# Attention scores by pairs of heads: the query's high and low part stacked on 128 rows, 128-column matmuls, and the last weight groups split at another place

## The chip, the cores and the metric

The kernel runs on one core of a Trainium2 chip. The metric is the device time of one execution in microseconds (us), the median of three runs: 1743.74 us before the change. Engines are named as the profile names them: PE (matmul, with PEld for its weight loads), DVE (vector), ACT (scalar), POOL (GpSimd) and SP, which issues nearly all the DMAs.

## The reference, cut to what matters

Two attention layers run one after the other. The change lies in the first: 4 x 1024 tokens of width 1024 look at 4 x 64 context rows, with 32 query heads of 32 columns and 8 key/value heads, each shared by 4 query heads.

```python
q = hidden_state @ Wq + bq                # 4096 x 1024
k = encoder_hidden_state @ Wk + bk        # 256 x 256
v = encoder_hidden_state @ Wv + bv
scores = jnp.einsum('bkgld,bksd->bkgls', q, k) * scale + mask
attn = jax.nn.softmax(scores, axis=-1)
out = jnp.einsum('bkgls,bksd->bkgld', attn, v)
x = layernorm(out @ Wo + bo + hidden_state) * gamma + beta
```

The second layer is an attention of 16 heads with 64 keys on x and the same context. The kernel keeps float32 accuracy by splitting each operand of a product into a high part, rounded to the TensorE's float32r type, and a low part (the rest), and adding three matmuls: high by low, low by high, high by high.

## The kernel before, in words

The first layer's attention is cut into 64 units (`UNITS`): a unit is one block of 512 tokens and one key/value head with its four query heads, so 128 rows of query. Eight units with the same tokens follow each other. Every engine runs one loop over slots `u`, written out by hand with semaphores; a slot holds steps of several units at once:

- PE, slot u: the query projection of unit u (`query`: 8 pieces of 3 matmuls of 512 columns, the helper `three`, whose lines are L53 to L55), between its pieces the product of attention and values of unit u-4 (`values_of`, 6 matmuls of 512 columns), and, behind piece 6, the scores of unit u-1: for each of 4 groups of 128 tokens one `three` of 256 columns, 12 matmuls. `qs` (the query, high and low tile) is the stationary side, `kb` the moving one. `kb` is block diagonal: head j's rows hold the keys in head j's 64 columns and zeros elsewhere.
- ACT: the exponential of unit u-2, the rounding of the next tokens' tile (`xT`), the copy of a finished output (`ot`), `qs` high from PSUM with the bias added (L869), then the rounding of the turned probabilities (`pT`).
- DVE: the sum of the exponentials of unit u-2 (L1107), a reciprocal, in even slots the turning of an input tile (L1040), the masked scores of unit u-1 out of PSUM (L1127) and their maximum (L1133), the turned probabilities of unit u-2 (L1138), `qs` low (L1142, `SCALAR_TENSOR_TENSOR`); in odd slots the low part of the input tile (L1047) comes first.
- POOL: low part of `pT` (L1381), scaling (L1385) and centering (L1390) of the probabilities.

PE waits for `qs` low of unit u-1 before its scores. One pair of slots (an even and an odd one) holds one input tile.

Ahead of the units the keys are rounded into `kst` (ACT the high plane at L839, DVE the low one at L1087), stored to DRAM (L288), and loaded for each unit into `kb` (L301, four DMAs, one for each head). The weight of the query projection `wq` comes in 8 column groups; a group is split by ACT (L793) and DVE (L1059) where `wq_early` and `wq_late` say, the last two in slot 1. The output projection's weight `wo` is split in the same way in the slots 57 to 64 (`wo_groups`; DVE L1064), and from slot 64 on `half_tile` multiplies by it: its second half waits for all 8 groups.

## Time and profile before

| what | value |
|---|---|
| median of 3 runs | 1743.74 us (1743.04 to 1747.58) |
| the profiled execution's own time | 1745.89 us |
| its span, first to last instruction | 1744.1 us |
| PE busy | 1712.8 us (98%), 8449 matmuls |
| DVE, POOL, ACT busy | 1165.5 (67%), 1066.8 (61%), 581.5 us (33%) |
| granted PE clock, mean | 0.995 |

The chain of work that ended last is 72% PE, 9% DVE, 8% POOL. A matmul's recorded time holds its way through the array; how fast matmuls follow each other is read from their starts. The units lie between about 31 and 575 us; behind them come the output projection with layer norm, the second layer's tables, and the second layer.

### The profile page before, as it was taken

Reading aid. Unit: us, or ns where it says so; the run is one execution under the profiler, and the core shown is the slowest. Engines: PE = TensorE matmul, PEld = TensorE weight load, DVE = VectorE, ACT = ScalarE, POOL = GpSimd, SP = SyncE. Lnnn points to the kernel's source line nnn. Section 1 sums busy time; section 2 is a strip of 40 time slices with the busy share of each in tenths; the row PEclk is TensorE's granted clock in tenths of the full one; section 3 lists DMA queues with packets and bytes.
Section 4 is the critical chain, followed back from the end, with each engine's and each line's share of the span. In section 5 each row is a group of like instructions: output and inputs, shape, how many; then the busy total and the mean of one; then the engine's idle time right before and its main releaser. Section 6 shows DMA issues by size and latency. Waiting matters only on the chain.

```text
span 1744.1 us, 22384 instructions
## 1 busy us (share of the span) xinstructions
PE 1712.8 (98%) x8449; PEld 1429.8 (82%) x8449; DVE 1165.5 (67%) x1106; ACT 581.5 (33%) x669; POOL 1066.8 (61%) x592
## 2 busy tenths in 40 slices
PE   6999999999999999999999999999999999999998
PEld 6788888888888788888888877888888888888887
DVE  7899888888888666565656578446644664466443
ACT  4344454444444533333434223122312231223110
POOL 1677878777788966575756553445734573457331
PEclk9999999999999999999999999999999999999999
DMA  8342344323335677777776856556545654565332
GB/s 238 99 111 73 88 104 105 85 71 86 80 81 162 198 237 223 227 231 222 248 219 224 263 176 194 174 169 185 173 152 169 185 170 154 169 183 171 130 110 84
DMA packets 278127, 280.11 MB, mean 161 GB/s; under 512 B 62330, under 2 KB 230404, under 8 KB 278020
## 3 DMA queue, kind: packets, MB, share of 16 engines
q1 hardware_dynamic: 276672, 276.97, 52.3%
q10 hardware_dynamic: 1348, 1.71, 0.3%
q8 instruction: 67, 1.10, 0.3%
q14 instruction: 40, 0.33, 0.1%
HBM read 175.81 MB, written 102.76 MB: 160 GB/s over the span
## 4 chain that ended last, share of the span: by engine, by line
PE 72%; DVE 9%; POOL 8%; issue 4%; ACT 3%; DMA 2%; SPq 1%; POOLq 0%; DVEq 0%; ACTq 0%
PE ps L53 23%; PE ps L54 23%; PE ps L55 23%; POOL pT0l L1381 2%; POOL pr L1385 1%; PE ps L712 1%; PE ps L720 1%; POOL xb L1407 1%; DVE pT1r L1138 1%; DVE pr L1127 1%; DVE small L1107 1%; DVE pT0r L1138 1%; ACT pT1h L881 1%; DVE xT1r L1040 1%; DVE xT0r L1040 1%
## 5 line engine op out<-in xcount | busy, mean ns | idle before, releaser
L1458 POOL TENSOR_TENSOR x2Tl<-x2r,x2Th 128x1024 fp32r<-128x1024 f32 x31 | 74.6, 2405 | 274.2 <-ACT x2Th L973 274.2
L1235 DVE STREAM_TRANSPOSE x2r<-xd 128x1024 f32<-128x1024 f32 x32 | 68.9, 2154 | 200.1 <-PE ps L55 200.1
L1390 POOL TENSOR_TENSOR pr<-pr,small 128x1024 f32<-128x1024 f32 x64 | 122.0, 1906 | 98.6 <-DVE small L1133 98.5
L973 ACT CAST x2Th<-x2r 128x1024 fp32r<-128x1024 f32 x32 | 33.7, 1053 | 366.5 <-DVE x2r L1235 366.5
L1385 POOL TENSOR_TENSOR pr<-pr,small 128x1024 f32<-128x1024 f32 x64 | 122.0, 1906 | 8.7 <-DVE small L1111 6.2
L1407 POOL TENSOR_TENSOR xb<-xb,bo 128x1024 f32<-128x1024 f32 x32 | 77.9, 2436 | 69.2 <-DMA xb<-in_x_dram 69.2
L1107 DVE TENSOR_REDUCE small<-pr 128x16 f32<-128x1024 f32 x64 | 78.0, 1219 | 45.7 <-ACT pr L852 45.7
L1421 POOL TENSOR_TENSOR y<-y,bet 128x1024 f32<-128x1024 f32 x31 | 74.4, 2400 | 55.7 <-DVE y L1153 55.7
L53 PE MATMUL ps<-wo0h,oc0l 128*128 128x512 f32 x256 | 101.7, 397 | 1.7 <-DVE wo0l L1064 1.7
L1153 DVE TENSOR_TENSOR y<-y,gam 128x1024 f32<-128x1024 f32 x32 | 56.0, 1751 | 70.6 <-ACT y L894 70.6
L53 PE MATMUL ps<-wo0h,oc1l 128*128 128x512 f32 x256 | 101.6, 397 | 0.4 <-DVE y L1190 0.4
L53 PE MATMUL ps<-xT0h,wq0l 128*128 128x512 f32 x256 | 100.8, 394 | 1.1 <-DVE wq0l L1059 1.1
L54 PE MATMUL ps<-xT0l,wq0h 128*128 128x512 f32 x256 | 100.7, 393 | 0.0
L55 PE MATMUL ps<-xT0h,wq0h 128*128 128x512 f32 x256 | 100.1, 391 | 0.0
L53 PE MATMUL ps<-xT1h,wq0l 128*128 128x512 f32 x256 | 100.0, 391 | 0.0
L54 PE MATMUL ps<-xT1l,wq0h 128*128 128x512 f32 x256 | 100.0, 391 | 0.0
L54 PE MATMUL ps<-wo0l,oc0h 128*128 128x512 f32 x256 | 99.8, 390 | 0.0
L54 PE MATMUL ps<-wo0l,oc1h 128*128 128x512 f32 x256 | 99.8, 390 | 0.0
L55 PE MATMUL ps<-wo0h,oc0h 128*128 128x512 f32 x256 | 99.7, 390 | 0.0
L55 PE MATMUL ps<-wo0h,oc1h 128*128 128x512 f32 x256 | 99.7, 390 | 0.0
L55 PE MATMUL ps<-xT1h,wq0h 128*128 128x512 f32 x256 | 99.6, 389 | 0.0
L1381 POOL TENSOR_TENSOR pT0l<-pT0r,pT0h 128x1024 fp32r<-128x1024 f32 x32 | 92.1, 2880 | 8.8 <-ACT pT0h L881 8.8
(379 smaller groups left out, 5446.3 us busy)
## 6 DMA issues: line engine op xcount, KB each, us to landing
xr<-in_x_dram SPq DMA_DIRECT2D x128, 128.0 KB, 2.9
o_scratch<-ot SPq DMA_DIRECT2D x256, 64.0 KB, 1.8
ocr<-o_scratch SPq DMA_DIRECT2D x16, 1024.0 KB, 7.9
xb<-in_x_dram SPq DMA_DIRECT2D x32, 512.0 KB, 6.2
a_scratch<-ost SPq DMA_DIRECT2D x64, 256.0 KB, 3.4
b_scratch<-ost SPq DMA_DIRECT2D x64, 256.0 KB, 5.6
xd<-x_scratch SPq DMA_DIRECT2D x128, 128.0 KB, 2.9
raw<-b_scratch SPq DMA_DIRECT2D x64, 256.0 KB, 5.9
```

Source lines behind the costliest of these rows:

```text
L53: nc.tensor.matmul(out, a[1], b[0], start=start, stop=False)
L54: nc.tensor.matmul(out, a[0], b[1], start=False, stop=False)
L55: return nc.tensor.matmul(out, a[0], b[0], start=False, stop=stop)
L1107: nc.vector.tensor_reduce(sm, pr[v % 2][:].rearrange("p j m s -> p (j m) s"), AX_X, ALU.add)\
L1153: nc.vector.tensor_tensor(y[n % 3][:], y[n % 3][:], gam0[:], ALU.mult).then_inc(scaled, 1)
L1235: nc.vector.transpose(x2r[:].rearrange("p k (t j) -> p t k j", t=TPB), xd[:].rearrange("p t (i k) -> p t k i", k=KT)).then_inc(x2_turned, 1)
L1381: nc.gpsimd.tensor_tensor(pT[v % 2][1][:], pTr[v % 2][:], f32(pT[v % 2][0][:]), ALU.subtract).then_inc(p_lo, 1)
L1385: nc.gpsimd.tensor_tensor(heads(v), heads(v), rs.unsqueeze(2).to_broadcast([P, TPB * GRP, KEYS]), ALU.mult)\
L1390: nc.gpsimd.tensor_tensor(heads(v), heads(v), mx.unsqueeze(2).to_broadcast([P, TPB * GRP, KEYS]), ALU.subtract)\
L1407: nc.gpsimd.tensor_tensor(xb[n % 2][:], xb[n % 2][:], bo0[:], ALU.add).then_inc(xbo, 1)
L1421: nc.gpsimd.tensor_tensor(y[n % 3][:], y[n % 3][:], bet0[:], ALU.add).then_inc(normed, 1)
L1458: nc.gpsimd.tensor_tensor(x2T[1][:], x2r[:], f32(x2T[0][:]), ALU.subtract).then_inc(x2_lo, 1)
```

## The change

The query tile of a unit is no longer a high and a low tile of four heads. Tile a holds heads 0 and 1: their high part on rows 0 to 63, their low part on rows 64 to 127. Tile b holds heads 2 and 3: high on rows 64 to 127, low on rows 0 to 63. ACT writes the two high halves and DVE the two low halves, with the low half going to the other 64 rows. Scores are formed by pairs of heads: for each of 4 token groups and each pair two matmuls of 128 columns, the first with low keys under the high rows only, the second with high keys under all rows. That is 16 matmuls of 128 columns in place of 12 of 256. `kst` has four planes (low, high, high, low), `kb` four planes of two heads, and each load of `kb` brings three planes.

The split of `wq` groups 6 and 7 goes from slot 1 to slots 3 and 5. The split of `wo` group 7 goes from slot 64 to slot 63.

```diff
-        kst = [at(f"kst{h}", 136 + 2 * h, [P, BATCH, 2, KEYS], F32R) for h in range(2)]
+        kst = [at(f"kst{h}", 130 + 4 * h, [P, BATCH, 4, KEYS], F32R) for h in range(2)]
-        kb = [at(f"kb{i}", 160 + 2 * i, [P, GRP, 2, KEYS], F32R) for i in range(2)]
+        kb = [at(f"kb{i}", 160 + 2 * i, [P, 4, 2, KEYS], F32R) for i in range(2)]
         def wq_late(u):
-            return (4, 5) if u == 0 else (6, 7) if u == 1 else ()
+            return (4, 5) if u == 0 else (6,) if u == 3 else (7,) if u == 5 else ()
         def wo_groups(u):
-            return (u - (UNITS - 7),) if UNITS - 7 <= u <= UNITS else ()
+            return (u - (UNITS - 7),) if UNITS - 7 <= u < UNITS else ()
...
                 for j in range(GRP):
-                    sp.dma_start(f32(kb[u % 2][32 * j:32 * (j + 1), j]).rearrange("p x s -> p (x s)"),
-                                 d["kv"][g // 4, t // 2, :, g % 4, :P]).then_inc(k_ld[u % 2], 16)
+                    x = 1 - j // 2
+                    sp.dma_start(f32(kb[u % 2][32 * j:32 * (j + 1), x:x + 3, j % 2]),
+                                 d["kv"][g // 4, t // 2, :, g % 4, KEYS * x:KEYS * (x + 3)].rearrange("p (x s) -> p x s", x=3))\
+                        .then_inc(k_ld[u % 2], 16)
...
                     for m in range(TPB):
-                        last = three(nc, S[v % 2][:, 256 * m:256 * (m + 1)], [qs[v % 2][x][:, m] for x in (0, 1)],
-                                     [kb[v % 2][:, :, x] for x in (0, 1)], True, True)
+                        for h in range(2):
+                            for x in (3 - 3 * h, 1 + h):
+                                last = nc.tensor.matmul(S[v % 2][:, 256 * m + P * h:][:, :P], qs[v % 2][h][:, m],
+                                                        kb[v % 2][:, x].rearrange("p j s -> p (j s)"), start=x in (0, 3), stop=x in (1, 2))
...
-                    nc.scalar.activation(qs[u % 2][0][:], Q[u % 2].rearrange("p (n m) -> p m n", m=TPB), ACT.Identity,
-                                         bias=bq[:, u % KT:u % KT + 1]).then_inc(q_hi, 1)
+                    for h in range(2):
+                        own = slice(64 * h, 64 * (h + 1))
+                        nc.scalar.activation(qs[u % 2][h][own], Q[u % 2][own].rearrange("p (n m) -> p m n", m=TPB), ACT.Identity,
+                                             bias=bq[own, u % KT:u % KT + 1]).then_inc(q_hi, 1)
...
-                    dve.wait_ge(q_hi, u + 1)
-                    nc.vector.scalar_tensor_tensor(out=qs[u % 2][1][:], in0=Q[u % 2].rearrange("p (n m) -> p m n", m=TPB), scalar=bq[:, u % KT:u % KT + 1],
-                                                   in1=f32(qs[u % 2][0][:]), op0=ALU.add, op1=ALU.subtract).then_inc(q_lo, 1)
+                    for h in range(2):
+                        own, other = slice(64 * h, 64 * (h + 1)), slice(64 * (1 - h), 64 * (2 - h))
+                        dve.wait_ge(q_hi, 2 * u + h + 1)
+                        nc.vector.scalar_tensor_tensor(out=qs[u % 2][h][other], in0=Q[u % 2][own].rearrange("p (n m) -> p m n", m=TPB),
+                                                       scalar=bq[own, u % KT:u % KT + 1], in1=f32(qs[u % 2][h][own]),
+                                                       op0=ALU.add, op1=ALU.subtract).then_inc(q_lo, 1)
```

On PE, the end of a unit's scores and the query projection behind them stand like this before (a row is an engine's instruction: line, operation, out<-in, shape; ps is PSUM, kb the keys, qs the query, xT the tokens; the first three rows of kb stand four times in a unit):

```order
L53 MATMUL ps<-kb_81,qs0l 128x256
L54 MATMUL ps<-kb_81,qs0h 128x256
L55 MATMUL ps<-kb_81,qs0h 128x256
L53 MATMUL ps<-xT0h,wq0l 128x512
L54 MATMUL ps<-xT0l,wq0h 128x512
```

and like this now (the first two rows stand four times in a unit, each for two matmuls):

```order
L657 MATMUL ps<-kb_81,qs0a 128x128 x2
L657 MATMUL ps<-kb_81,qs0b 128x128 x2
L53 MATMUL ps<-xT0h,wq0l 128x512
L54 MATMUL ps<-xT0l,wq0h 128x512
L55 MATMUL ps<-xT0h,wq0h 128x512
```

Nothing else on PE has moved; a unit has four instructions more there.

On DVE, slots 1 and 2 (the low query of unit 1 to the low query of unit 2 and the first low part of slot 3; pr are the scores of a unit, pT the turned probabilities, small holds maxima and sums) stand like this before:

```order
L1142 SCALAR_TENSOR_TENSOR qs1l<-ps,small,qs1h 128x512
L1059 TENSOR_TENSOR wq0l<-wq0r,wq0h 128x8x128 x2
L1107 TENSOR_REDUCE small<-pr_85 128x16
L1111 RECIPROCAL small<-small 128x16
L1040 STREAM_TRANSPOSE xT1r<-xr_59 128x4x8x32
L1127 TENSOR_TENSOR pr_86<-ps,mask_95 128x4x4x64
L1133 TENSOR_REDUCE small<-pr_86 128x16
L1138 STREAM_TRANSPOSE pT0r<-pr_85 128x16x2x32
L1142 SCALAR_TENSOR_TENSOR qs0l<-ps,small,qs0h 128x512
L1047 TENSOR_TENSOR xT1l<-xT1r,xT1h 128x8x128
```

and like this now:

```order
L1152 SCALAR_TENSOR_TENSOR qs1a<-ps,small,qs1a 64x512
L1152 SCALAR_TENSOR_TENSOR qs1b<-ps,small,qs1b 64x512
L1115 TENSOR_REDUCE small<-pr_85 128x16
L1119 RECIPROCAL small<-small 128x16
L1047 STREAM_TRANSPOSE xT1r<-xr_59 128x4x8x32
L1135 TENSOR_TENSOR pr_86<-ps,mask_95 128x4x4x64
L1141 TENSOR_REDUCE small<-pr_86 128x16
L1146 STREAM_TRANSPOSE pT0r<-pr_85 128x16x2x32
L1152 SCALAR_TENSOR_TENSOR qs0a<-ps,small,qs0a 64x512
L1152 SCALAR_TENSOR_TENSOR qs0b<-ps,small,qs0b 64x512
L1054 TENSOR_TENSOR xT1l<-xT1r,xT1h 128x8x128
```

The two splits of wq are gone from this place (one stands behind the low query of unit 3, one behind that of unit 5), and each low query is two instructions of 64 rows.

On DVE, at the seam of the units and the output projection (slots 63 and 64; wo0l is the low part of a group of wo), the rows before are:

```order
L1142 SCALAR_TENSOR_TENSOR qs1l<-ps,small,qs1h 128x512
L1064 TENSOR_TENSOR wo0l<-wo0r,wo0h 128x8x128
L1107 TENSOR_REDUCE small<-pr_85 128x16
L1111 RECIPROCAL small<-small 128x16
L1127 TENSOR_TENSOR pr_86<-ps,mask_96 128x4x4x64
L1133 TENSOR_REDUCE small<-pr_86 128x16
L1138 STREAM_TRANSPOSE pT0r<-pr_85 128x16x2x32
L1064 TENSOR_TENSOR wo0l<-wo0r,wo0h 128x8x128
```

and now:

```order
L1152 SCALAR_TENSOR_TENSOR qs1a<-ps,small,qs1a 64x512
L1152 SCALAR_TENSOR_TENSOR qs1b<-ps,small,qs1b 64x512
L1071 TENSOR_TENSOR wo0l<-wo0r,wo0h 128x8x128 x2
L1115 TENSOR_REDUCE small<-pr_85 128x16
L1119 RECIPROCAL small<-small 128x16
L1135 TENSOR_TENSOR pr_86<-ps,mask_96 128x4x4x64
L1141 TENSOR_REDUCE small<-pr_86 128x16
L1146 STREAM_TRANSPOSE pT0r<-pr_85 128x16x2x32
```

The last group of wo stands five instructions earlier, ahead of the sum, the masked scores and the turned probabilities of the last units.

## Rows read from the trace of the kernel before

**Rows 1.** The page: busy us, share of the span, instructions of each engine.
```profile
PE 1712.8 (98%) x8449; PEld 1429.8 (82%) x8449; DVE 1165.5 (67%) x1106; ACT 581.5 (33%) x669; POOL 1066.8 (61%) x592
```
**Rows 2.** Busy time by stage: us, PE, PEld, DVE, ACT, POOL, PEclk, DMA share, GB/s.
```profile
72.00:294.00 222.00, 222.00 (x1128) 189.81 (x1127) 197.37 (x193) 100.60 (x124) 172.96 (x84) 1.00 0.38 97
```
**Rows 3.** What PE waited for: us in total, times, longest us.
```profile
PE ps L53 <- DVE qs0l L1142: 6.1, 5, 3.8
PE ps L53 <- DVE wo0l L1064: 1.7, 1, 1.7
```
**Rows 4.** Timeline of PE in the units: start us, us, engine, line, operation.
```profile
79.08 0.28 PE L53 MATMUL ps<-kb,qs0l 128*128 128x256 f32 x1
...
293.84 0.28 PE L53 MATMUL ps<-kb,qs0l 128*128 128x256 f32 x1
...
300.06 0.39 PE L53 MATMUL ps<-pT0h,vb 128*128 128x512 f32 x1
...
302.11 0.29 PE L53 MATMUL ps<-kb,qs1l 128*128 128x256 f32 x1
...
303.54 0.40 PE L53 MATMUL ps<-xT0h,wq0l 128*128 128x512 f32 x1
```
**Rows 5.** Timeline of PEld behind a wait, the scores of unit 32.
```profile
311.07 0.19 PEld L53 LDWEIGHTS ps<-kb,qs0l 128*128 128x128 f32 x1 [0.97 <-DVE qs0l L1142]
311.18 0.19 PEld L54 LDWEIGHTS ps<-kb,qs0h 128*128 128x128 f32 x1
311.30 0.19 PEld L55 LDWEIGHTS ps<-kb,qs0h 128*128 128x128 f32 x1
```
**Rows 6.** 128-column transposes on PE, timeline, and durations (min/median/max ns) by line.
```profile
620.78 1.04 PE L693 MATMUL ps<-ident,wo1r 128*128 128x128 f32 x8
...
L693 PE MATMUL ps<-ident,wo1r x64: 272/273/273, 620.8 to 947.6; 128*128 128x128 f32 x64
```
**Rows 7.** Groups of PEld by line: busy us, mean ns, idle before.
```profile
L55 PEld LDWEIGHTS ps<-kb,qs0h 128*128 128x128 f32 x128 | 25.0, 195 | 0.0
```
**Rows 8.** Timeline of DVE over a pair of slots.
```profile
219.73 1.22 DVE L1107 TENSOR_REDUCE small<-pr 128x16 f32<-128x1024 f32 x1 [1.45 <-ACT pr L852]
...
226.72 0.71 DVE L1142 SCALAR_TENSOR_TENSOR qs0l<-ps,small,qs0h 128x512 fp32r<-128x512 f32 x1
227.35 1.37 DVE L1047 TENSOR_TENSOR xT1l<-xT1r,xT1h 128x1024 fp32r<-128x1024 f32 x1
228.88 1.22 DVE L1107 TENSOR_REDUCE small<-pr 128x16 f32<-128x1024 f32 x1 [0.16 <-ACT pr L852]
...
236.21 1.22 DVE L1107 TENSOR_REDUCE small<-pr 128x16 f32<-128x1024 f32 x1 [1.45 <-ACT pr L852]
```
**Rows 9.** Timeline of ACT ahead of the last of these rows.
```profile
235.12 1.06 ACT L852 ACTIVATE pr<-pr 128x1024 f32<-128x1024 f32 x1
```
**Rows 10.** The first units: the chain (start us, us), timelines of four engines, and a window.
```profile
36.30 2.19 DMA kv_scratch<-kst
...
39.84 0.42 SPq L301
...
41.84 0.28 PE L53 MATMUL ps<-kb,qs0l 128*128 128x256 f32 x1
...
46.10 1.91 POOL L1390 TENSOR_TENSOR pr<-pr,small 128x1024 f32<-128x1024 f32 x1 [19.67 <-DVE small L1133]
...
49.66 2.36 DVE L1059 TENSOR_TENSOR wq0l<-wq0r,wq0h 128x1024 fp32r<-128x1024 f32 x2 [2.99 <-ACT wq0h L793]
...
59.64 0.58 PE L53 MATMUL ps<-kb,qs0l 128*128 128x256 f32 x1 [3.85 <-DVE qs0l L1142]
...
60.00:70.00 10.00, 10.00 (x39) 8.52 (x39) 8.21 (x10) 3.70 (x5) 9.26 (x5) 0.71 0.29 79
```
**Rows 11.** The seam to the output projection, timeline of DVE and PE.
```profile
574.78 1.74 DVE L1064 TENSOR_TENSOR wo0l<-wo0r,wo0h 128x1024 fp32r<-128x1024 f32 x1
...
576.58 0.50 PE L53 MATMUL ps<-wo0h,oc0l 128*128 128x512 f32 x1 [1.72 <-DVE wo0l L1064]
```

More of the change, by code:

```diff
@@ L98, in program @@
         wv = [at("wv0h", 184, [P, KT, KV0], F32R), at("wv0l", 152, [P, KT, KV0], F32R)]
-        kst = [at(f"kst{h}", 136 + 2 * h, [P, BATCH, 2, KEYS], F32R) for h in range(2)]
+        kst = [at(f"kst{h}", 130 + 4 * h, [P, BATCH, 4, KEYS], F32R) for h in range(2)]
         vst = [at(f"vst{r}", 140 + 2 * r, [P, KVH0, 2, HD0], F32R) for r in range(2)]
         kf, vf = at("kf", 202, [P, 2, CTX]), at("vf", 204, [P, 2, KV0])
-        qs = [[at(f"qs{i}{x}", 152 + 4 * i + 2 * j, [P, TPB, P], F32R) for j, x in enumerate("hl")] for i in range(2)]
-        kb = [at(f"kb{i}", 160 + 2 * i, [P, GRP, 2, KEYS], F32R) for i in range(2)]
+        qs = [[at(f"qs{i}{x}", 152 + 4 * i + 2 * j, [P, TPB, P], F32R) for j, x in enumerate("ab")] for i in range(2)]
+        kb = [at(f"kb{i}", 160 + 2 * i, [P, 4, 2, KEYS], F32R) for i in range(2)]
         vb = [at(f"vb{i}", 164 + 2 * i, [P, 2, 2, P], F32R) for i in range(2)]
@@ L616, in query @@
                             pe.wait_ge(x_lo, 4 * (t + 1))
-                        after(pe, q_lo, u - 1)
+                        after(pe, q_lo, 2 * (u - 1))
                     for k in ks:
@@ L643, in slot @@
                     if u < UNITS:
-                        pe.wait_ge(q_lo, v + 1)
+                        pe.wait_ge(q_lo, 2 * (v + 1))
                     pe.wait_ge(k_ld[v % 2], 16 * GRP * (v // 2 + 1))
@@ L673, in half_tile @@
                     if h == 0:
-                        pe.wait_ge(q_lo, UNITS - 1)
+                        pe.wait_ge(q_lo, 2 * (UNITS - 1))
                     after(pe, y_done, h - 1)
@@ L838, in scalar @@
                 act.wait_ge(kfull, h + 1)
-                nc.scalar.copy(kst[h][:, :, 0, :].rearrange("p b (r i) -> p b r i", r=2),
-                               kf[:, h].rearrange("p (r b i) -> p b r i", r=2, b=BATCH)).then_inc(k_hi, 1)
+                for x in (1, 2):
+                    last = nc.scalar.copy(kst[h][:, :, x, :].rearrange("p b (r i) -> p b r i", r=2),
+                                          kf[:, h].rearrange("p (r b i) -> p b r i", r=2, b=BATCH))
+                last.then_inc(k_hi, 1)
             split_wq(1)
@@ L868, in slot @@
                     after(act, scores, u - 1)
-                    nc.scalar.activation(qs[u % 2][0][:], Q[u % 2].rearrange("p (n m) -> p m n", m=TPB), ACT.Identity,
-                                         bias=bq[:, u % KT:u % KT + 1]).then_inc(q_hi, 1)
+                    for h in range(2):
+                        own = slice(64 * h, 64 * (h + 1))
+                        nc.scalar.activation(qs[u % 2][h][own], Q[u % 2][own].rearrange("p (n m) -> p m n", m=TPB), ACT.Identity,
+                                             bias=bq[own, u % KT:u % KT + 1]).then_inc(q_hi, 1)
                     for g in wq_late(u):
                         split_wq(g)
+                    if u == UNITS - 1:
+                        split_wo(KT - 1)
                     if u - 2 * KT in (6, 7):
                         norm_rows(u - 2 * KT - 6)
-                if u == UNITS:
-                    for g in wo_groups(u):
-                        split_wo(g)
                 if 2 <= u < UNITS + 2:
@@ L1086, in vector @@
                 dve.wait_ge(k_hi, h + 1)
-                nc.vector.tensor_tensor(kst[h][:, :, 1, :].rearrange("p b (r i) -> p b r i", r=2),
-                                        kf[:, h].rearrange("p (r b i) -> p b r i", r=2, b=BATCH),
-                                        f32(kst[h][:, :, 0, :]).rearrange("p b (r i) -> p b r i", r=2), ALU.subtract)\
-                    .then_inc(k_lo, 1)
+                for x in (0, 3):
+                    last = nc.vector.tensor_tensor(kst[h][:, :, x, :].rearrange("p b (r i) -> p b r i", r=2),
+                                                   kf[:, h].rearrange("p (r b i) -> p b r i", r=2, b=BATCH),
+                                                   f32(kst[h][:, :, 1, :]).rearrange("p b (r i) -> p b r i", r=2), ALU.subtract)
+                last.then_inc(k_lo, 1)
             dve.wait_ge(bv_ld, 16)
@@ L1140, in slot @@
                 if u < UNITS:
-                    dve.wait_ge(q_hi, u + 1)
-                    nc.vector.scalar_tensor_tensor(out=qs[u % 2][1][:], in0=Q[u % 2].rearrange("p (n m) -> p m n", m=TPB), scalar=bq[:, u % KT:u % KT + 1],
-                                                   in1=f32(qs[u % 2][0][:]), op0=ALU.add, op1=ALU.subtract).then_inc(q_lo, 1)
+                    for h in range(2):
[4 more added lines that the diff above has]
+                                                       op0=ALU.add, op1=ALU.subtract).then_inc(q_lo, 1)
                 for g in wq_late(u):
                     split_wq(g)
-                if wo_groups(u):
-                    split_wo(u - (UNITS - 7))
+                for g in wo_groups(u):
+                    split_wo(g)
+                if u == UNITS - 1:
+                    split_wo(KT - 1)
                 if u in range(KT + 3, KT + 11, 2):
@@ L1530, in build @@
         "x2": nc.dram_tensor("x2_scratch", [TOKENS, D], F32).ap(),
-        "kv": nc.dram_tensor("kv_scratch", [2, BATCH, HD0, GRP, 2 * P], F32).ap(),
+        "kv": nc.dram_tensor("kv_scratch", [2, BATCH, HD0, GRP, 3 * P], F32).ap(),
         "a": nc.dram_tensor("a_scratch", [BATCH, D, D], F32).ap(),
```

8 lines of the change are left out of this document (4 added, 4 removed).

## The prediction

> **What bounds the kernel now.** I read the busy shares first: PE is busy 98% of the span, DVE 67% [rows 1]. That average hides the stage that the change touches, so next I looked at the stage. Between 72 and 294 us, in the units, PE is never idle, but DVE is busy 197.4 of 222 us, 89% [rows 2]: two engines near their limit, not one. The list of waits shows PE held by the low query 6.1 us in 5 waits, 3.8 us of it in one, and 1.7 us once by the last group of wo [rows 3]. So PE sets the time, and DVE is close behind.
>
> The period of a unit comes from the starts of its scores: unit 4 at 79.08, unit 30 at 293.84, 26 units, 8.260 us each [rows 4]. It is made of 30 matmuls of 512 columns and 12 of 256. From 300.06 to 302.11 nine of 512 start, 0.228 us apart; from 302.11 to 303.54 the twelve scores, 1.43 us or 119 ns each [rows 4]. Per column that is 213/512 and 107/256 at the 2.4 GHz granted here (PEclk 1.00 in [rows 2]), and in both some 13 ns more.
>
> DVE's own loop: in a pair of slots it goes from one sum of exponentials (219.73) to the same place two slots on (236.21), 16.48 us; two PE periods are 16.52 us [rows 8]. Inside, DVE waits only for the exponential: 0.16 us ahead of one sum, 1.45 us ahead of the other. The second wait has a reason: ACT's exponential starts at 235.12, takes 1.06 and ends at 236.18, and the sum starts at 236.21 [rows 8, 9]. ACT turns to it after the cast of the turned probabilities, so this wait runs from DVE's own transpose, whatever DVE does in between.
>
> **The scores on PE.** Twelve matmuls go (1.43 us a unit), sixteen of half the columns come. By columns alone one would be 53 + 13 = 66 ns, 16 of them 1.06 us, a gain. But each brings its own weight load. Behind a wait, where no matmul is in the way, the second load of 128 rows starts 0.11 us after the first [rows 5], and eight transposes of 128 columns, each with a load, follow each other every (1.04 - 0.27)/7 = 0.110 us [rows 6]. A load that repeats the weights of the matmul ahead is not skipped: L55 uses the same high query as L54 and still loads it for 195 ns, of which most overlaps [rows 7]. So I take 109 ns for one: 16 x 109 = 1.744 us, 0.31 us a unit more, over 64 units +19.9 us. The bounds: 66 ns if loads hid fully, and 119 ns, what the wider matmul takes, since a narrower one can hardly take longer; that is 1.90 us, +0.47 a unit, +30 us.
>
> The page "TensorE: Matmul & The Clock Gate" of the Trainium skill, section "LDWEIGHTS (loading the stationary operand)", speaks against this change in the same way: a load takes its columns divided by 1.2 GHz, an estimate of 107 ns for 128, against 0.11 us in [rows 5]; the trace agrees.
>
> **The low query on DVE and the high one on ACT.** Each becomes two instructions of 64 rows and the same 512 elements. Nothing in the trace shows 64 rows on these engines. If rows cost nothing and elements all, the second is worth a full one: 0.63 us from its start to the next one's (226.72 to 227.35, [rows 8]). If time went with rows, the pair would cost what one does, +0. I take the first, since a duration here follows the elements of a row: 0.71 for 512, 1.37 for 1024 [rows 8]. On ACT, which is busy 45% in this stage [rows 2], the second half lies in idle time. On DVE it counts by slot. In the slot with the 1.45 us wait it is hidden, as 0.63 is less. In the other it adds 0.63 less the 0.16 of wait there: 0.47 to the pair, 16.95 us. PE's pair becomes 2 x 8.26 + 0.62 = 17.14. So PE stays the bound, by 0.19 us a pair.
>
> That margin could go. DVE's instructions now overlap by 0.71 - 0.63 = 0.08 us [rows 8]. The Trainium skill's "VectorE: DVE Perf Modes", section "Two Vector instructions with no wait between them", says that an instruction waits for all earlier ones to finish when its first input or its output begins in another group of 32 partitions than before; here the write to the other half, the step to the second half and the step back would each be held. By that rule the pair would be 16.95 + 3 x 0.08 = 17.19, DVE would bind by 0.05 a pair, and the sum would rise by an estimated 1.6 us. No row of before has such a step, so the trace neither bears it out nor denies it.
>
> **The start.** Before, scores of unit 2 waited until 59.64; the query matmul ahead had its slot at 55.41 + 0.23, so 4.0 us were lost, and PE's clock then fell: the mean granted from 60 to 70 is 0.71, some 2.9 us more [rows 10]. In slot 1 DVE waited 2.99 us and split groups 6 and 7 for 2.36 us, to 52.02. Without them its next step, the sum, waits for POOL's centering (46.10 + 1.91 = 48.01) and the exponential (1.06), so it can begin at 49.1, 2.9 us earlier; the second low query of unit 2 takes 0.6 of that back. PE wants the result as before, a little later by its own longer scores. The wait shrinks to 4.0 - 2.3 - 0.2 = 1.5 us, and after a wait of 1.7 us elsewhere (576.58, [rows 11]) PE went on at once, so I leave the fall of the clock out. Against this stands the first load of keys: stored bytes double. The store's landing of 2.19 us at 36.30 leads to the loads, the fourth issued from 39.84 to 40.26, and PE starts on them at 41.84 without a wait [rows 10]; I see no slack there. Two more splits of keys on DVE (0.35 us ahead of the first store), a longer landing (between +0 and +2.2, I take 0.6) and three planes for two in the load (0.2) make 1.2 us of wait at unit 0, between 0.4 and 2.8. Sum of the start: 1.5 + 1.2 - 4.0 - 2.9 = -4.2 us, between -6 and -1.
>
> **The middle.** Groups 6 and 7 are now split in slots 3 and 5, 1.2 us of DVE each, where 1.45 - 0.63 = 0.8 us lies idle: 0.4 each reaches PE. The four shorter waits of before (6.1 - 3.8 = 2.3 us, [rows 3]) had up to 0.5 us of slack ahead that is now used up; I add 1.2 us. Sum +2.0, between 0 and +4.
>
> **The seam.** wo's last group was ready at 576.5, and PE waited 1.72 us for it [rows 11]; five instructions earlier this is gone. But 1.4 us of split and 0.6 of query now stand ahead of the last units' scores on DVE, and POOL and the last products come behind those. I give back half: -1.0, between -1.8 and +1.
>
> **Sum.** 19.9 - 4.2 + 2.0 - 1.0 = +16.7 us. The profiled execution took 1745.89 us (span 1744.1), 2.15 us over the median of the runs; it would become 1762.6, and the median 1743.74 becomes 1760.4. I say 1760 us.
>
> **The rivals.** First, the matmul costs its upper bound, 119 ns: +30.1, with DVE's margin wide enough that the middle adds nothing: 30.1 - 4.2 - 1.0 = +25, 1769 us. For it speaks that every float32r matmul in this trace has its 13 ns on top; against it the transposes at 110.
>
> Second, DVE becomes the bound: the second low query counts in both slots, because the longer work pushes the transposes and with them the exponential. The pair is 16.48 + 2 x 0.63 = 17.74, 0.61 a unit over 8.26: 64 x 0.61 = 39, less 4.2, plus 2, less 1: +36, 1780 us. Against it stands the order on ACT, by which the exponential does not wait for the low query.
>
> Third, loads hide behind each other and a matmul costs 66 to 85 ns. PE's unit would shrink to 7.9 or 8.2 us, but then DVE's 16.95 a pair binds: 0.215 a unit, +13.8 - 4.2 + 2.0 - 1.0 = +10.6, 1754 us. The Trainium skill's "TensorE: Matmul & The Clock Gate", section "Back-to-back issue gap", gives 81 ns for a stream of loads and 128-column matmuls, by which PE alone would gain 0.14 us a unit; [rows 5, 6] show no such pair under 110.
>
> Fourth, and faster: a matmul under 90 ns (1.43/16) and two half-sized low queries for the price of one. Both must hold; then DVE's loop stays 16.48, no gain is left in the units, and the start and the seam bring 1743.7 - 5.2 = 1738.5 us. It decides only below 90 ns and below 0.04 us for the second low query.
>
> **How the numbers follow.** Forecast 0.61 (its own span 1752 to 1767), first rival 0.15, second 0.10, third 0.09, fourth 0.05. A range of 1750 to 1777 leaves out the second and the fourth, and tails of the start. Some 0.3% (5.2 us) is what a measurement of this kernel can tell from no change. The fourth rival lies on that edge, so half of it is faster and half the same; some of the third with a better start joins the same: faster 0.03, same 0.04, slower 0.93.
>
> **What will show it.** The 16 score matmuls should start 109 ns apart, 1.74 us a unit, and the starts of scores lie 8.57 us apart in the middle of the units. If the spacing is 67, PE should wait in every other unit for the second low query. If it is 119, the starts lie 8.73 apart with fewer waits. DVE's low queries should take 0.71 us each, and the wait ahead of every second sum should fall from 1.45 to about 0.8. At the start no drop of the clock near 60 us; at the seam no wait for wo. I am wrong if a 128-column matmul of this type costs something that loads and columns don't show, or if 64 rows cost half.

## The result, and the profile after

The changed kernel takes 1816.88 us (median of 6 runs, 1815.78 to 1817.73) against 1744.38 us before (also of 6; the 1743.74 of above was the median of the first three): a ratio of 1.0407, 95% interval 1.0396 to 1.0418, 72.5 us slower. Slower was forecast, but by 16.7 us, and the time lies far outside the range of 1750 to 1777.

The page of the changed kernel (busy us and shares as in [rows 1], then the chain of work that ended last):

```profile
PE 1749.3 (96%) x8705; PEld 1450.3 (80%) x8705; DVE 1273.0 (70%) x1172; ACT 633.9 (35%) x735; POOL 1056.4 (58%) x592
...
PE 56%; DVE 20%; issue 12%; POOL 6%; ACT 3%; DMA 2%; SPq 1%; POOLq 0%; DVEq 0%; ACTq 0%
```

The span grew by 70.8 us to 1814.9, PE's busy time by only 36.5. DVE grew by 107.5, and its share of the chain from 9% to 20%. The changed kernel's list of waits (us in total, times, longest), beside [rows 3]:

```profile
PE ps L657 <- DVE qs1b L1152: 22.2, 26, 2.8
PE ps L657 <- DVE qs0b L1152: 17.9, 25, 2.8
...
PE ps L586 <- ACT normTr L816: 2.2, 1, 2.2
```

Before, PE waited 5 times for the low query; now 51 times of 64, 40.1 us in total. The windows of the changed kernel, beside [rows 2] and the last row of [rows 10]:

```profile
60.00:70.00 10.00, 9.19 (x52) 7.65 (x50) 9.80 (x9) 4.43 (x5) 6.49 (x4) 1.00 0.42 106
...
72.00:294.00 222.00, 208.82 (x1064) 174.12 (x1063) 213.90 (x193) 107.54 (x132) 146.00 (x74) 0.98 0.34 85
```

In the units PE is no longer always busy (208.8 of 222 us). DVE nearly is, with 213.9, or 96%. So DVE became the bound. PE's own part stands in its timeline (start us, us; x2 is two matmuls in a row), beside [rows 4]:

```profile
244.46 0.33 PE L657 MATMUL ps<-kb,qs1a 128*128 128x128 f32 x2
...
246.20 0.45 PE L53 MATMUL ps<-xT0h,wq0l 128*128 128x512 f32 x1
246.49 0.40 PE L54 MATMUL ps<-xT0l,wq0h 128*128 128x512 f32 x1
```

Sixteen score matmuls fill 246.20 - 244.46 = 1.74 us, as forecast. The first wide matmul behind them is followed after 0.29 us, not after 0.23 as elsewhere; that was not in the sum.

Now DVE and POOL over the even half of a pair, in the changed kernel's timeline, beside [rows 8]:

```profile
508.16 1.22 DVE L1115 TENSOR_REDUCE small<-pr 128x16 f32<-128x1024 f32 x1 [0.51 <-ACT pr L858]
...
514.13 1.23 DVE L1146 STREAM_TRANSPOSE pT0r<-pr 128x1024 f32<-128x1024 f32 x1
515.39 0.74 DVE L1152 SCALAR_TENSOR_TENSOR qs0a<-ps,small,qs0a 64x512 fp32r<-64x512 f32 x1
516.17 0.76 DVE L1152 SCALAR_TENSOR_TENSOR qs0b<-ps,small,qs0b 64x512 fp32r<-64x512 f32 x1
516.95 3.02 DVE L1054 TENSOR_TENSOR xT1l<-xT1r,xT1h 128x1024 fp32r<-128x1024 f32 x1
519.90 1.21 DVE L1115 TENSOR_REDUCE small<-pr 128x16 f32<-128x1024 f32 x1
...
516.53 2.37 POOL L1394 TENSOR_TENSOR pT0l<-pT0r,pT0h 128x1024 fp32r<-128x1024 f32 x1 [0.33 <-ACT pT0h L888]
```

Between the turned probabilities and the input tile's low part lie 2.82 us now (514.13 to 516.95). And that low part, 1.37 us in [rows 8], takes 3.02. From sum to sum this half is 11.74 us, the pair 18.97 (500.93 to 519.90) where PE needs two times 8.65 (e3 below). Before, POOL's instruction of the same kind started 0.61 us behind DVE's 227.35 of [rows 8]; two more rows of DVE from that pair of slots, and the timeline of POOL, in the kernel before:

```profile
225.56 1.23 DVE L1138 STREAM_TRANSPOSE pT0r<-pr 128x1024 f32<-128x1024 f32 x1
...
232.88 1.25 DVE L1138 STREAM_TRANSPOSE pT1r<-pr 128x1024 f32<-128x1024 f32 x1 [0.17 <-POOL pr L1385]
...
227.96 3.02 POOL L1381 TENSOR_TENSOR pT0l<-pT0r,pT0h 128x1024 fp32r<-128x1024 f32 x1 [0.33 <-ACT pT0h L881]
```

There POOL was the one that took 3.02 instead of the 2.40 that it takes in the other slot. The two have changed places.

**Theory 1:** these two instructions keep each other out. Whichever starts first runs through, and the other ends only when both are done. The longer low query turned their order round. **Theory 2:** the added DVE time costs by itself, the longer low part is a by-product. **Theory 3:** PE's matmuls, or the moved groups, are the cost.

### The profile page after: what moved, and what is told of

It is laid out like the page before. It is cut to its first block, busy times and chain, and to the rows that moved or that the text cites. A ratio compares the mean times of both kernels' runs of the same rounds, so it can differ in the third digit from the quotient of the medians.

```text
span 1814.9 us, 23028 instructions
## 1 busy us (share of the span) xinstructions
PE 1749.3 (96%) x8705; PEld 1450.3 (80%) x8705; DVE 1273.0 (70%) x1172; ACT 633.9 (35%) x735; POOL 1056.4 (58%) x592
## 4 chain that ended last, share of the span: by engine, by line
PE 56%; DVE 20%; issue 12%; POOL 6%; ACT 3%; DMA 2%; SPq 1%; POOLq 0%; DVEq 0%; ACTq 0%
PE ps L53 18%; PE ps L54 17%; PE ps L55 17%; DVE small L1115 4%; DVE pr L1135 4%; DVE pT1r L1146 2%; DVE pT0r L1146 2%; PE ps L716 1%; PE ps L724 1%; ACT pT1h L888 1%; ACT pr L858 1%; DVE qs0b L1152 1%; DVE qs0a L1152 1%; POOL pr L1398 1%; POOL pT0l L1394 1%
## 5 line engine op out<-in xcount | busy, mean ns | idle before, releaser
L1166 DVE TENSOR_TENSOR y<-y,gam 128x1024 f32<-128x1024 f32 x32 | 56.9, 1777 | 72.5 <-ACT y L901 72.5
L1203 DVE TENSOR_TENSOR y<-ps,xb 128x512 f32<-128x512 f32 x64 | 43.8, 684 | 69.7 <-PE ps L55 66.4
```

## The experiments

**e1_pool_waits**: POOL is made to wait, nothing else.

```diff
+                    if u <= UNITS and (n := next_x(u - 1)) is not None:
+                        pool.wait_ge(x_lo, n + 1)
                     pool.wait_ge(p_hi, v + 1)
```

> The changed kernel with one wait added: GpSimd's low part of the turned probabilities starts only after VectorE's low part of the input tile, in the slots that have one; nothing else is moved. Theory 1 (whichever of the two starts first keeps the other out until it ends, and the second low-query instruction has turned their order round): the input tile's low part takes 1.2 to 1.4 us instead of 3.02, GpSimd's instruction about 2.4, VectorE's pair of units 17.1 to 17.6 us instead of 18.97, total 1765 to 1785 us against 1816.9. Theory 2 (the extra VectorE instruction costs by its own time alone) and theory 3 (the 128-column matmuls bind): no change or slower, 1815 or above.

Measured: 1790.56 us, ratio 1.0269 (1.0253 to 1.0284). Timeline of DVE and POOL:

```profile
512.85 1.23 DVE L1054 TENSOR_TENSOR xT1l<-xT1r,xT1h 128x1024 fp32r<-128x1024 f32 x1
...
518.46 1.25 DVE L1146 STREAM_TRANSPOSE pT1r<-pr 128x1024 f32<-128x1024 f32 x1 [0.46 <-POOL pr L1400]
...
514.16 2.41 POOL L1396 TENSOR_TENSOR pT0l<-pT0r,pT0h 128x1024 fp32r<-128x1024 f32 x1 [2.07 <-DVE xT1l L1054]
```

An added wait made the kernel 26 us faster: theories 2 and 3 have no place for that. The low part takes 1.23 us. The total is 5.6 us over theory 1's range, and the pair 17.77 (504.02 to 521.79): POOL, sent back, delivers its scaled probabilities late, and DVE waits 0.46 us for them.

**e2_split_early**: DVE's low part of the input tile goes behind the maximum of the slot before.

```diff
-                if 1 <= u <= UNITS and (n := next_x(u - 1)) is not None:
-                    split_x(n)
...
                     nc.vector.tensor_reduce(mx, ..., ALU.max).then_inc(maxed, 1)
+                if u < UNITS and (n := next_x(u)) is not None:
+                    split_x(n)
```

> The changed kernel with VectorE's low part of the input tile moved half a unit earlier: behind the maximum of the same slot and ahead of the turned probabilities, instead of behind the two low-query instructions. Theory 1: it leaves the collision with GpSimd's low part of the probabilities, but meets GpSimd's centring, which is released at the same moment, so that one of these two waits: the pair is 17.5 to 18.6 us, total 1775 to 1805. Theory 2: the same instructions in another order, total 1815 +- 5. Theory 3: no change.

Measured: 1796.36 us, ratio 1.0301 (1.0285 to 1.0316). Timeline:

```profile
515.31 1.22 DVE L1054 TENSOR_TENSOR xT1l<-xT1r,xT1h 128x1024 fp32r<-128x1024 f32 x1
...
515.47 2.82 POOL L1403 TENSOR_TENSOR pr<-pr,small 128x1024 f32<-128x1024 f32 x1 [2.60 <-DVE small L1139]
```

As theory 1 expected: DVE first by 0.16 us, its instruction is short and POOL's centering takes 2.82 instead of 1.91. The same instructions in this order are 20 us faster.

**e3_whole_query**: PE's part and the moves without the two halves; ACT and DVE each make the query with one instruction of 128 rows again.

```diff
-                    for h in range(2):
-                        ... scalar_tensor_tensor(out=qs[u % 2][h][other], in0=Q[u % 2][own] ...
+                    nc.vector.scalar_tensor_tensor(out=qs[u % 2][1][:], in0=Q[u % 2] ...
```

> The changed kernel with the query's high and its low part each made by one instruction on 128 rows, as before, while TensorE still runs the 16 matmuls of 128 columns a unit (on parts that are not the pairs' stacked halves, so that the scores are not the reference's). It is TensorE's part of the change without VectorE's. Theories 1 and 2: VectorE's pair goes back to 16.5 us and TensorE binds at 17.1 to 17.3 a pair, the input tile's low part takes 1.4 us: total 1750 to 1765. Theory 3: TensorE's matmuls are the cost, total above 1800.

Measured: 1764.99 us, ratio 1.0117 (1.0102 to 1.0132). Windows, and starts of scores two units apart on PE's timeline:

```profile
72.00:294.00 222.00, 222.00 (x1183) 190.46 (x1181) 190.78 (x188) 96.81 (x119) 169.87 (x83) 1.00 0.39 97
```

```profile
500.41 0.33 PE L657 MATMUL ps<-kb,qs1a 128*128 128x128 f32 x2
...
517.71 0.33 PE L657 MATMUL ps<-kb,qs1a 128*128 128x128 f32 x2
```

PE is always busy again, at (517.71 - 500.41)/2 = 8.65 us a unit. This is the time that the prediction forecast, 1765 against 1760, but only without the two halves. Theory 3 falls: PE's part and the moves by themselves cost 21 us, not 72.

**e4_before_low_twice**: the reverse, DVE's part alone in the kernel before. The low query is computed twice, the second time behind a wait for the first.

```diff
+                    for h in range(2):
+                        dve.wait_ge(q_lo, 2 * u + h) if u + h else None
                         nc.vector.scalar_tensor_tensor(out=qs[u % 2][1][:], ...).then_inc(q_lo, 1)
```

> The kernel before with the low-query instruction (128 rows, 0.71 us) run twice into the same tile, its 12 matmuls of 256 columns and all else unchanged. It is VectorE's part of the change without TensorE's. Theory 1: the input tile's low part now starts behind GpSimd's and takes 3.0 us; VectorE's pair 18.7 to 19.0 us, total 1795 to 1815. Theory 2 (own time alone): pair 16.48 + 2 x 0.75 - 1.0 = 17.0 us against TensorE's 16.5 to 16.9, total 1750 to 1765. Theory 3: within 5 us of 1744.

Measured: 1803.93 us, ratio 1.0341 (1.0324 to 1.0358): one more instruction of 0.7 us a unit costs 60 us, with PE's work as before. Timeline:

```profile
505.57 3.31 DVE L1047 TENSOR_TENSOR xT1l<-xT1r,xT1h 128x1024 fp32r<-128x1024 f32 x1
...
505.40 2.40 POOL L1384 TENSOR_TENSOR pT0l<-pT0r,pT0h 128x1024 fp32r<-128x1024 f32 x1 [0.33 <-ACT pT0h L881]
```

POOL is ahead by 0.17 us, and that is enough.

**e5_two_moves**: e1 and one move more, the turning of the input tile behind the scores' addition.

```diff
                         .then_inc(s_read, 1)
+                    if turn is not None:
+                        turn_x(turn)
                     dve.wait_ge(s_read, v + 1)
```

> The changed kernel with GpSimd's wait of the first experiment, and VectorE's turning of the input tile moved from ahead of the scores' addition to behind it, into a stretch in which GpSimd is idle. Theory 1, as it now stands (each collision with GpSimd lengthens VectorE by what is left of GpSimd's instruction; the pair was 17.77 us with the first wait): the turning takes 1.2 instead of 2.15 us, VectorE's pair would be 16.9, so TensorE binds at 2 x 8.647 = 17.29 a pair in most pairs; total 1765 to 1778. Rival (VectorE's halves bind by their own time and the held issue): the period stays at 8.72 or above, total 1788 or more.

Measured: 1794.57 us, ratio 1.0293 (1.0273 to 1.0313). A miss: the time lies in the rival's range (1788 or more), and 4 us above that of e1. Timeline:

```profile
509.82 2.19 DVE L1047 STREAM_TRANSPOSE xT1r<-xr 128x1024 f32<-128x1024 f32 x1
...
508.53 1.91 POOL L1403 TENSOR_TENSOR pr<-pr,small 128x1024 f32<-128x1024 f32 x1
```

The turning takes 2.19 us although POOL is done 0.62 us into it. Ahead of the units, four turnings in a row take 8.19 us in the kernel before, 2.05 each, the first two with POOL idle. So an instruction of this kind takes some 2.1 us by itself: I had counted a collision where there was none. The rival, that DVE's halves bind by their own time, is not refuted by this run.

**e6_old_matmuls_on_halves**: the halves, with the 12 matmuls of before.

```diff
-                            for x in (3 - 3 * h, 1 + h):
-                                last = nc.tensor.matmul(S[v % 2][:, 256 * m + P * h:][:, :P], ...)
+                        last = three(nc, S[v % 2][:, 256 * m:256 * (m + 1)], ...)
```

> The changed kernel with the query still made in halves by two instructions on each engine, but TensorE running the 12 matmuls of 256 columns a unit of before on those tiles (so that the scores are not the reference's). Theory 1: VectorE's loop binds, the pair stays near 18.9 us, total 1800 to 1815 in spite of TensorE's shorter work. Theory 3 (TensorE's matmuls are the cost): total near 1750.

Measured: 1819.48 us (one run), 4 us over theory 1's range. DVE's low part of the tile stands there with 3.05 us. With the cheaper PE work of before the time is no better than the changed kernel's 1816.88: there PE's form costs nothing that this run shows, it lies behind DVE.

**e7_64_columns**: each score matmul cut in two.

```diff
+                            for j in range(2):
-                                last = nc.tensor.matmul(S[v % 2][:, 256 * m + P * h:][:, :P], ...)
+                                    last = nc.tensor.matmul(S[v % 2][:, 256 * m + P * h + KEYS * j:][:, :KEYS], ...)
```

> The changed kernel with each score matmul of 128 columns cut into two of 64 columns, 32 a unit, the computation unchanged. If a matmul with a weight load of its own costs a fixed time that its columns don't set: 32 x 0.109 = 3.5 us a unit instead of 1.74, TensorE's work 10.4 us a unit, total 1860 to 1880. If the columns set it: about 1.75 us a unit as now and a total within 10 us of 1817.

Measured: 1880.05 us (one run), at the upper edge of the first range. PE's timeline, where no wait stands:

```profile
505.53 0.53 PE L658 MATMUL ps<-kb,qs0a 128*128 128x64 f32 x4
...
509.02 0.48 PE L53 MATMUL ps<-xT1h,wq0l 128*128 128x512 f32 x1
509.33 0.40 PE L54 MATMUL ps<-xT1l,wq0h 128*128 128x512 f32 x1
```

Thirty-two of them take 509.02 - 505.53 = 3.49 us, 109 ns each, exactly as long as those of 128 columns. So columns don't set the time of either; at these two widths a matmul with a weight load of its own costs a fixed time. That it is the load and nothing else was not tried. The wide matmul behind them again has 0.31 us.

**e8_before_moves_only** and **e10_before_query_groups**: the kernel before with both moves of weight groups, and with the first alone.

```diff
-            return (4, 5) if u == 0 else (6, 7) if u == 1 else ()
+            return (4, 5) if u == 0 else (6,) if u == 3 else (7,) if u == 5 else ()
...
-            return (u - (UNITS - 7),) if UNITS - 7 <= u <= UNITS else ()
+            return (u - (UNITS - 7),) if UNITS - 7 <= u < UNITS else ()
...
+                if u == UNITS - 1:
+                    split_wo(KT - 1)
```

> The kernel before with only the moved weight groups of the change (the sixth and seventh group of the query's weights split in slots 3 and 5, the last group of the output's weights split in slot 63), scores as before. By the prediction's working: start -4.2 with +2.0 for the slots that take the groups, seam -1.0, so 1740 to 1743. Rival (the moved groups meet GpSimd on VectorE, as in the changed kernel where units 4 and 6 stalled by 3 us each): 1744 to 1750.

> The kernel before with only the sixth and seventh group of the query's weights split in slots 3 and 5, the output's groups as before. In the run with both moves the scores of the units came 4.6 us earlier from unit 3 on and 4 us were lost again at the seam, where TensorE waited twice for GpSimd's low probabilities and once for the first norm's columns. If the seam's loss is the output group's move: 1738 to 1740.5, faster than both kernels. If the tail takes back whatever the start gives: 1743 to 1745.

Measured: 1743.17 us for both moves, ratio 0.9992 (0.9983 to 1.0002), no difference, and between the two ranges; 1742.10 us for the query groups alone, ratio 0.9984 (0.9974 to 0.9993), just faster than before, by less than the 0.3% that the prediction took as the least to be told from no change, and again between the two ranges. From unit 3 on the scores start 4.6 and 4.7 us earlier, and those of the last unit still 4.6 (563.9 for 568.5); so the gain is lost behind the units, most of it with both moves and about half with the query groups alone. PE's waits at the seam with both moves:

```profile
PE ps L584 <- ACT normTr L812: 2.2, 1, 2.2
PE ps L53 <- POOL pT0l L1382: 2.0, 1, 2.0
```

The wait for wo's last group (1.7, [rows 3]) is gone, and these two stand in its place: the seam gives nothing. And with the query groups alone the start of unit 2 shows what the first move does: a wait of 1.58 us for 3.85 in [rows 10], and a granted clock of 1.00 from 60 to 70 us for 0.71:

```profile
57.76 0.35 PE L53 MATMUL ps<-kb,qs0l 128*128 128x256 f32 x1 [1.58 <-DVE qs0l L1142]
```

```profile
60.00:70.00 10.00, 10.00 (x51) 8.53 (x50) 9.45 (x10) 4.08 (x5) 9.18 (x5) 1.00 0.29 83
```

**e12_query_groups_back**: the opposite in the changed kernel (the first line of that diff turned round).

> The changed kernel with the sixth and seventh group of the query's weights split in slot 1 again, as before the change. Theory 1: the groups in slots 3 and 5 make VectorE late behind GpSimd, so that units 4 and 6 start 3 us late each; with the groups back unit 3 loses its 4 us gain again and the stalls of units 4 to 7 (10 us in the changed kernel) go: total 1808 to 1815. Rival (the move is worth its forecast gain in both kernels): 1818 to 1823.

Measured: 1814.29 us, ratio 1.0401 (1.0387 to 1.0415), against 1.0407 (1.0396 to 1.0418): the intervals overlap, so the total doesn't decide. It lies in theory 1's range, 2.6 us below the changed kernel. The traces show the shift: unit 4 is no longer held up by 2.8 us, but unit 2 waits 4.44 us for the 2.23 of the changed kernel. In the changed kernel the move gains 5.1 us by unit 3 (its scores start at 68.92, here at 73.99) and has lost them and 4.1 more by unit 7 (114.00 and 109.93), since the moved group meets POOL too. The changed kernel's timeline, slot 5:

```profile
90.28 3.04 DVE L1066 TENSOR_TENSOR wq0l<-wq0r,wq0h 128x1024 fp32r<-128x1024 f32 x1
...
89.86 2.38 POOL L1394 TENSOR_TENSOR pT1l<-pT1r,pT1h 128x1024 fp32r<-128x1024 f32 x1 [0.34 <-ACT pT1h L888]
```

**e9_half_dose**: e4 with the second instruction on half of the columns.

> The kernel before with the low-query instruction repeated on half of its columns (256 of 512, an estimated 0.4 us instead of 0.7), nothing else changed: half the dose of the fourth experiment, which was 60 us slower. Theory 1 (who starts first): in the kernel before VectorE's low part of the input tile starts 0.61 us ahead of GpSimd's instruction, so 0.4 us leaves it ahead and nothing turns round: the input tile's low part stays at 1.3 to 1.4 us, TensorE still binds at 8.26 a unit, total 1742 to 1752. Theory 2 (cost in proportion to VectorE's time): about half of the 60 us, total 1768 to 1780.

Measured: 1755.11 us, ratio 1.0064 (1.0049 to 1.0080). Timeline:

```profile
504.30 1.22 DVE L1047 TENSOR_TENSOR xT1l<-xT1r,xT1h 128x1024 fp32r<-128x1024 f32 x1
...
509.69 1.25 DVE L1138 STREAM_TRANSPOSE pT1r<-pr 128x1024 f32<-128x1024 f32 x1 [0.42 <-POOL pr L1388]
...
504.39 3.40 POOL L1384 TENSOR_TENSOR pT0l<-pT0r,pT0h 128x1024 fp32r<-128x1024 f32 x1 [0.33 <-ACT pT0h L881]
```

Half the dose costs 11 us, not 30: DVE is still first, by 0.09 us, and its low part stays short. It is a step, not a slope. Theory 1's range is missed by 3 us, since POOL, the loser here, took 3.40 and then held DVE up by 0.42 us for its scaled probabilities.

**e11_rows_kept** and **e13_own_rows**: what makes the two halves dear. In the first both lie on rows 0 to 63; in the second each stays on its own rows, and only the step from the first half to the second, and back, is left.

```diff
-                                                       ... out=qs[u % 2][h][other], in0=Q[u % 2][own] ...
+                                                       ... out=qs[u % 2][h][:64], in0=Q[u % 2][:64] ...
```

```diff
-                                                       ... out=qs[u % 2][h][other], in0=Q[u % 2][own] ...
+                                                       ... out=qs[u % 2][1 - h][own], in0=Q[u % 2][own] ...
```

> The changed kernel with both halves of the query made on rows 0 to 63 and left there (no step to other rows), VectorE's two instructions behind both of ScalarE's, and the score matmuls on 64 rows, so that the scores are not the reference's. If the step to other rows makes the half dearer than the whole (0.75 and a step of 0.78 us against 0.71): VectorE's two instructions fall to about 0.71 each, overlapping the transposes before them again, and the collision stays: total 1805 to 1812. If any two instructions on half of the rows cost that: within 4 us of 1816.

> The changed kernel with each half's low query left on the rows of its own half (in the other half's tile, so that all tiles are full and the 16 matmuls unchanged, but the scores are not the reference's), VectorE's two instructions behind both of ScalarE's. In the changed kernel the input tile's low part starts 1.26 + 0.78 + 0.78 = 2.82 us after the turned probabilities, GpSimd 2.40 us after them. If the step from input rows to output rows within one instruction costs the hold: none is held, 1.16 + 0.63 + 0.65 = 2.44 us, level with GpSimd as with the rows kept, the input tile's low part takes 1.2 us and TensorE binds at 8.647: total 1765 to 1775. If each change of rows from one instruction to the next costs it: the second and the instruction behind it are held, 1.16 + 0.77 + 0.78 = 2.71 us, GpSimd is 0.3 us ahead, the collision stays: total 1808 to 1816.

Measured: 1784.99 us (one run) and 1817.48 us, ratio 1.0418 (1.0399 to 1.0436). Timelines of DVE and POOL, first with the rows kept:

```profile
505.24 1.23 DVE L1145 STREAM_TRANSPOSE pT0r<-pr 128x1024 f32<-128x1024 f32 x1
506.40 0.70 DVE L1150 SCALAR_TENSOR_TENSOR qs0a<-ps,small,qs0a 64x512 fp32r<-64x512 f32 x1
507.03 0.73 DVE L1150 SCALAR_TENSOR_TENSOR qs0b<-ps,small,qs0b 64x512 fp32r<-64x512 f32 x1
507.68 1.21 DVE L1053 TENSOR_TENSOR xT1l<-xT1r,xT1h 128x1024 fp32r<-128x1024 f32 x1
...
507.64 3.50 POOL L1392 TENSOR_TENSOR pT0l<-pT0r,pT0h 128x1024 fp32r<-128x1024 f32 x1 [0.33 <-ACT pT0h L887]
```

then with each half on its own rows:

```profile
513.90 1.23 DVE L1146 STREAM_TRANSPOSE pT0r<-pr 128x1024 f32<-128x1024 f32 x1
515.06 0.70 DVE L1152 SCALAR_TENSOR_TENSOR qs0b<-ps,small,qs0a 64x512 fp32r<-64x512 f32 x1
515.79 0.76 DVE L1152 SCALAR_TENSOR_TENSOR qs0a<-ps,small,qs0b 64x512 fp32r<-64x512 f32 x1
516.58 3.18 DVE L1054 TENSOR_TENSOR xT1l<-xT1r,xT1h 128x1024 fp32r<-128x1024 f32 x1
...
516.29 2.37 POOL L1394 TENSOR_TENSOR pT0l<-pT0r,pT0h 128x1024 fp32r<-128x1024 f32 x1 [0.33 <-ACT pT0h L888]
```

The 1817.48 is 1.5 us over the range of e13's second reading and far from the first's. From the transposes to the low part: 2.44 us with the rows kept, 2.68 with the two changes of rows, 2.82 in the changed kernel with three. Steps between starts that keep the rows are 1.16, 0.63 and 0.65; those that change them 1.26, 0.78 and 0.78 in the changed kernel, 0.73 and 0.79 in e13. So each change of rows from one instruction to the next costs 0.10 to 0.15 us: the overlap of the two is lost. The Trainium skill's "VectorE: DVE Perf Modes", section "Two Vector instructions with no wait between them", gives a model for this: an instruction is held until all earlier ones are done when one of its inputs starts in another group of 32 partitions than the first input of the last instruction that read the same memory, or its output in another than the last output there. The traces agree. A fourth such step stands behind these: the masked scores, which DVE reads from PSUM from row 0 on after a second half read from row 64 on, start 0.28 us after the reciprocal (502.17 to 502.45 in the changed kernel) where it was 0.17 before (230.13 to 230.30). It does not touch the order with POOL, but adds 0.11 us to a slot; that the rows are its cause was not tried by itself. At 2.44 us DVE is level with POOL and keeps the way free; at 2.68 it isn't. My range for the rows kept was missed on the good side (1785 for 1805 to 1812), because I took the order to be lost there already. PE sets its time, 8.94 us a unit: the score matmuls on 64 rows start 0.32 us behind the wide matmul ahead of them, for 0.23 elsewhere (509.28 to 509.60), and the wide one behind them 0.21 after the last, for 0.12 (511.32 to 511.53; 246.08 to 246.20 in the changed kernel), which is this experiment's own cost.

**e14_pool_waits_all**: e1, and POOL waits for the splits of weight groups as well.

```diff
+                        for g in wq_late(u - 1):
+                            pool.wait_ge(wq_lo, g + 1)
+                        for g in wo_groups(u - 1):
+                            pool.wait_ge(wo_lo, g + 1)
```

> The first experiment's kernel, with GpSimd's low part of the turned probabilities also waiting for VectorE's split of a weight group where one stands ahead of it (query groups 6 and 7, all output groups). If these splits are the rest of the collision: they take 1.2 us instead of 3.04, the units 5 to 7 and 57 to 63 lose their stalls, some 3 and 6 us: total 1780 to 1784, against 1790.6 with the first wait alone. If GpSimd's lateness is what remains: its scaled probabilities come later in these slots too, and the total stays between 1787 and 1792.

Measured: 1781.06 us, ratio 1.0209 (1.0192 to 1.0226), as expected: the groups' splits are 1.23 us, and 9.5 us more come back.

## Why the prediction was wrong, point by point

**The step that failed** is the sentence on DVE: "In the other it adds 0.63 less the 0.16 of wait there: 0.47 to the pair, 16.95 us", and from it "PE stays the bound". It treated DVE's instructions behind the low query as fixed in length. One of them was not: 1.37 us when it starts 0.61 us ahead of POOL's, 3.02 when it starts 0.42 behind. The prediction's own prices used up that margin: before, the low part started 1.79 us after the transpose of the probabilities, and POOL's instruction 2.40 after it (225.56, 227.35 and 227.96). 1.79 + 0.63 = 2.42 makes the two level, and three steps of 0.08, which it weighed too, put DVE 0.26 behind. In the working stands another misreading of [rows 8]: DVE did not wait for the exponential alone, it also waited 0.17 us for POOL's scaled probabilities in the odd slot (232.88), the wait that is 0.46 in e1 and 0.42 in e9. For six kernels, start of DVE's low part less start of POOL's, and what the two took:

| kernel | DVE less POOL, us | DVE took | POOL took |
|---|---|---|---|
| before | -0.61 | 1.37 | 3.02 |
| e9 | -0.09 | 1.22 | 3.40 |
| e11 | +0.04 | 1.21 | 3.50 |
| e4 | +0.17 | 3.31 | 2.40 |
| e13 | +0.29 | 3.18 | 2.37 |
| changed | +0.42 | 3.02 | 2.37 |

Where DVE is late it ends 1.07 to 1.10 us behind POOL (changed kernel: 519.97 and 518.90), a little under its own 1.2; where POOL is late it ends 2.25 to 2.27 us behind DVE. They don't share, they take turns. The same stands in all 16 traces of this case, where a low part that DVE makes of an input tile or a weight group starts within 0.8 us of POOL's instruction 399 times between 50 and 720 us: in the 202 cases in which DVE starts first, or at most 0.05 us behind, it takes 1.37 us or less; in the 197 in which it starts 0.14 us behind or more, 3.0 or more. The turn goes over between the two. The Trainium skill's page "SBUF — State Buffer", section "SBUF: two separate sides", has this as an exclusive lock on a port pair of the two engines (on DVE's side for an instruction with two SBUF inputs), which whichever starts first keeps for its whole instruction. The traces agree with that but for the 0.04 us of e11, where POOL's record starts first and DVE still goes ahead. The sign stood in the trace before, in the 3.02 and 2.40 us of one line of POOL, and I did not ask what it was.

**The prices, one by one.** The second low query: 0.65 us by e11, forecast 0.63. The three changes of rows: 0.10 + 0.15 + 0.13 = 0.38 us, forecast 3 x 0.08, by a rule that I weighed and priced at 1.6 us in all; the 0.38 is what takes DVE from level with POOL to 0.42 late. The odd slot's wait fell from 1.45 to 0.51 us, forecast 0.8; so far, but for the steps between rows, DVE's own loop was understood.

**Where the 72 us are.** PE's part with the moves and whole queries: 21 (e3). Put on top of that, the halves cost the other 52, of which 26 come back when POOL is kept behind the input tile's low part (e1), 9.5 more when it is kept behind the weight groups' too (e14). The last 16 remain with POOL's wait in place; the 0.46 us a pair by which its probabilities are then late is the difference of 17.77 to 17.31 us, about PE's 17.29 a pair, and over some 31 pairs 14 us. That this is all of the 16 is argued from the trace, not tried, and the halves' own time with their held steps, the rival of e5, may be a part of it.

**PE** was right in kind and short in size: 109 ns a matmul (e7: fixed, not set by columns), but the first wide matmul behind the scores has 0.06 us more. 0.39 us a unit (8.647 for 8.260) instead of 0.31, 24.8 us instead of 19.9. Rivals one and three (119 ns, 66 to 85 ns) are out. Rival two had DVE as the bound at 17.74 a pair; the bound was right, its mechanism (both slots) not, and the 17.77 of e1 agrees with it only by chance. In the changed kernel PE's extra lies hidden behind DVE altogether (e6).

**The start**: -4.2 forecast, of it -5.4 for the moved groups and +1.2 for the keys. The groups gave -4.6 to -4.7 in the kernel before (e8, e10), and the clock did not fall: 1.00 from 60 to 70 us, in the changed kernel too. In the changed kernel unit 3 was 1.9 us early, and units 4 and 6 lost it behind POOL. The wait for the first keys, 1.2 forecast, is 0.8 us at unit 0, whose scores start at 42.21 instead of 41.84. **The middle**: +2.0 for two splits of 1.2 us in idle time; they took 3.02 and 3.04. **The seam**: the wait for wo went, two others of 2.0 and 2.2 us came (e8).

## What to carry to other kernels

Before an instruction is added to an engine, look whether the same instruction of a neighbour has two durations in the trace: if so, two engines may take turns there (the turning of e5 was a case where they don't), and the order of their starts, with its margin (0.61 us here), belongs in the sum. Here a loop in which DVE was 89% busy had no room for "hidden" work whose delay moved such a meeting, and a wait that keeps the better order brought back half of the loss (1817 to 1781 us). And narrower matmuls may save nothing: here one with a weight load of its own took 109 ns at 64 columns as at 128.

## What the runs showed that I had not expected

An added wait on one engine made the whole kernel 26 us faster (e1). A difference of 0.13 us between two starts decides over 2.1 us on DVE (1.21 in e11 and 3.31 in e4). Matmuls of 64 and of 128 columns take the same 109 ns (e7). In e7 the granted clock fell while PE was never idle, behind a unit's 32 matmuls of 64 columns (493.50 to 496.99). From 499.40 to 501.40 its mean is 0.56, so most of that stretch lay at the lower of the two levels, 1.2 GHz and 2.4. Wide matmuls start 0.43 us apart there (497.77 to 500.75, seven steps) where it is 0.23 at the higher:

```profile
499.40:501.40 2.00, 2.00 (x6) 1.53 (x5) 1.97 (x3) 1.80 (x3) 1.65 (x1) 0.56 0.16 31
```
